# Down projection of a decoder layer: a third buffer for rounded values, four output banks, and clamps six units ahead of the additions

## What is computed

```python
def _quant_act_int8(x):
    amax = jnp.maximum(jnp.quantile(jnp.abs(x), 1.0 - 0.005), 1e-5)
    s = 127 / amax
    return jnp.clip(jnp.round(x * s), -128, 127) / s

def _quant_w_ternary(w):
    gamma = jnp.mean(jnp.abs(w)) + 1e-5
    return jnp.clip(jnp.round(w / gamma), -1.0, 1.0) * gamma

h = layernorm(x, ln_g, ln_b)
h = einsum('btd,hd->bth', _quant_act_int8(h), _quant_w_ternary(w1))   # up, 256 -> 1024
h = gelu(h)
out = einsum('btd,hd->bth', _quant_act_int8(h), _quant_w_ternary(w2)) # down, 1024 -> 256
x = x + (x + out)          # this part; x already holds the two stages before
```

## Time and profile before

| | us |
|---|---|
| median of 3 runs (lowest 1035.44, highest 1038.0) | 1035.82 |
| the profiled execution, its time | 1035.35 |
| its span, from the first to the last instruction | 1033.5 |
| VectorE's first instruction of the down projection starts at | 980.90 |
| last addition starts at | 1029.88 |
| last output DMA is issued at | 1031.35 |

### The profile page before, as it was taken

The page is one execution under the profiler, slowest core; times in us unless marked ns, Lnnn a source line. Parts: engine busy times, 40 slices in busy tenths (PEclk is TensorE's granted clock), DMA queues, the critical chain, the costliest instruction groups (busy, mean ns, idle before and its releaser), DMA issues.

```text
span 1033.5 us, 19418 instructions
## 1 busy us (share of the span) xinstructions
PE 880.8 (85%) x6218; PEld 674.9 (65%) x6225; DVE 867.2 (84%) x2448; ACT 659.6 (64%) x1663; POOL 545.7 (53%) x499
## 2 busy tenths in 40 slices
PE   7798999999989999999899899888999922995275
PEld 7586777777777777877777677655666621542164
DVE  4689899999999989889998879856677787899887
ACT  4677677776667756757666566345677651894095
POOL 6355476476456646644664554355678870880000
PEclk9899999999999989989998899999999975998599
DMA  9800000000000000002100000140420000000012
GB/s 163 138 3 10 6 6 11 7 7 10 8 7 8 10 6 6 8 9 80 55 11 7 6 6 10 29 125 21 155 79 1 1 1 1 1 1 1 1 67 97
DMA packets 28572, 30.49 MB, mean 30 GB/s; under 512 B 5548, under 2 KB 23864, under 8 KB 28472
## 3 DMA queue, kind: packets, MB, share of 16 engines
q1 hardware_dynamic: 28256, 29.12, 11.3%
q10 hardware_dynamic: 216, 0.14, 0.0%
HBM read 20.85 MB, written 4.19 MB: 24 GB/s over the span
## 4 chain that ended last, share of the span: by engine, by line
DVE 43%; PE 40%; issue 9%; ACT 4%; POOL 3%; DVEq 0%; ACTq 0%; POOLq 0%
PE ps L1862 6%; DVE arena L1283 5%; DVE arena L1291 5%; PE ps L2048 4%; DVE arena L1344 3%; PE ps L1932 3%; DVE arena L1269 3%; DVE arena L1272 3%; PE psY L1900 3%; PE psX L2069 3%; PE psY L2069 2%; PE ps L2247 2%; DVE arena L1336 2%; PE psG L2048 2%; DVE arena L1264 2%
## 5 line engine op out<-in xcount | busy, mean ns | idle before, releaser
L509 POOL TENSOR_SCALAR_AFFINE_SELECT arena<-arena 128x2048 f32<-128x2048 f32 x32 | 64.4, 2013 | 269.2 <-DVE arena L1272 262.7
L524 POOL TENSOR_TENSOR work<-work,half 128x16 f32<-128x16 f32 x32 | 93.8, 2931 | 2.7
L1924 PE MATMUL ps<-work 32*128 32x256 f32 x512 | 84.6, 406 | 10.2 <-ACT arena L713 10.1
L513 POOL TENSOR_SCALAR_AFFINE_SELECT arena<-arena 128x2048 f32<-128x2048 f32 x32 | 92.1, 2877 | 2.2
L678 ACT ACTIVATE arena<-ps,nparity 32x256 f32<-32x256 f32 x124 | 51.1, 457 | 63.8 <-PE ps L1862 63.4
L1924 PEld LDWEIGHTS ps<-work 32*128 32x128 f32 x512 | 54.7, 186 | 45.4 <-issue 27.1
L713 ACT ACTIVATE arena<-ps 128x512 f32<-128x512 f32 x128 | 68.9, 589 | 14.1 <-PE ps L1924 13.7
L1862 PE MATMUL ps<-work,arena 128*128 128x64 f32 x496 | 61.4, 277 | 19.3 <-DVE work L1308 19.2
L1862 PEld LDWEIGHTS ps<-work,arena 128*128 128x128 f32 x496 | 58.7, 193 | 28.8 <-issue 28.6
L1900 PE MATMUL psY<-work,arena 128*128 128x96 f32 (+1 forms) x512 | 69.1, 301 | 5.6 <-DVE arena L1362 5.6
L1900 PEld LDWEIGHTS psY<-work,arena 128*128 128x128 f32 x512 | 67.5, 216 | 6.4 <-DVE arena L1362 6.4
(11 more groups left out here) (344 smaller groups left out, 2548.7 us busy)
## 6 DMA issues: line engine op xcount, KB each, us to landing
arena<-in_mask_BxSxS_ik SPq DMA_DIRECT2D x8, 1024.0 KB, 6.8
xs<-arena SPq DMA_DIRECT2D x256, 16.0 KB, 1.8
arena<-in_ctx SPq DMA_DIRECT2D x8, 512.0 KB, 4.3
out<-xs SPq DMA_DIRECT2D x32, 128.0 KB, 1.7
arena<-in_x SPq DMA_DIRECT2D x8, 288.0 KB, 18.0
arena<-in_L_ffn_w SPq DMA_DIRECT2D x2, 1024.0 KB, 22.0
arena<-in_x SPq DMA_DIRECT2D x16, 96.0 KB, 6.4
arena<-in_L_attn_w_qkvb SPq DMA_DIRECT2D x2, 512.0 KB, 5.0
```

What stands on the lines that cost most here:

```text
L509: G.affine_select(out=keys, in_=keys, compare_op=ALU.is_ge, fill=0.0, base=0, pattern=[[0, NH], [1, P]], channel_multiplier=-1).then_inc(h ...
L513: G.affine_select(out=pairs, in_=pairs, compare_op=ALU.is_ge, fill=0.0, base=0, pattern=[[0, NH], [-CT, B], [0, CT]], channel_multiplier=1 ...
L524: own(G.tensor_tensor(root, length, half, ALU.pow))
L1924: last = M.matmul(ps[(2, 0)[r % 2]][:, f * 2 * P:(f + 1) * 2 * P], kq[j % 4][rows, f * P:(f + 1) * P], qe[rows, f].rearrange("p e t -> p ( ...
```

## The change

`gq` gets a third buffer, in the space of `hq` and `hqT`. Block i uses buffer i % 3, and the writers of unit u wait only from u = 12 on, for block i - 3. The output banks are four, `psX`, `psY`, `ps[0]`, `ps[1]`, and unit n waits for the addition of unit n - 4. VectorE clamps units 1, 0, 3, 2, 4, 5 first, and then for each n unit n + 6 before it adds unit n. No instruction is added or removed but waits; what each computes is the same.

```diff
         hq = [take_work(FF // 2).bitcast(BF16) for _ in range(2)]
         hqT = [take_work(FF // 2).bitcast(BF16) for _ in range(2)]
+        assert at[0] == third_block + 2 * FF
+        gq.append(work[:, third_block:at[0]].bitcast(BF16))
...
+        def down_bank(n):
+            return (psX, psY, ps[0], ps[1])[n % 4][:, 0:D]
...
             def quantised_gelu(u):
                 act.wait_ge(gr_ready, on_act(u))
-                if u >= 8:
-                    act.wait_ge(down_mm, 4 * (u // 4 - 1))
-                A.activation(gq[u // 4 % 2][:, u % 4 * FF:(u % 4 + 1) * FF], gT[:, u * FF:(u + 1) * FF], ACT.Copy,
+                if u >= 12:
+                    act.wait_ge(down_mm, 4 * (u // 4 - 2))
+                A.activation(gq[u // 4 % 3][:, u % 4 * FF:(u % 4 + 1) * FF], gT[:, u * FF:(u + 1) * FF], ACT.Copy,
                              bias=-ROUND).then_inc(ga_ready, 1)
...
             def clamped(u):
-                t, q = gT[:, u * FF:(u + 1) * FF], gq[u // 4 % 2][:, u % 4 * FF:(u % 4 + 1) * FF]
+                t, q = gT[:, u * FF:(u + 1) * FF], gq[u // 4 % 3][:, u % 4 * FF:(u % 4 + 1) * FF]
...
-                if u >= 8:
-                    v.wait_ge(down_mm, 4 * (u // 4 - 1))
+                if u >= 12:
+                    v.wait_ge(down_mm, 4 * (u // 4 - 2))
...
             def added(n):
                 v.wait_ge(down_mm, n + 1)
                 xt = xs[:, n, :]
-                V.scalar_tensor_tensor(xt, psO[n % 2], deq[:, 1:2], xt, ALU.mult, ALU.add).then_inc(out_ready, 1)
+                V.scalar_tensor_tensor(xt, down_bank(n), deq[:, 1:2], xt, ALU.mult, ALU.add).then_inc(out_ready, 1)
...
-            for u in (1, 0, 3, 2):
+            for u in (1, 0, 3, 2, 4, 5):
                 clamped(u)
             for n in range(NT):
-                if n + 4 < NT:
-                    clamped(n + 4)
+                if n + 6 < NT:
+                    clamped(n + 6)
                 added(n)
...
                 if r == 0:
                     pe.wait_ge(gd_ready, 4 * (i + 1))
-                if n >= 2:
-                    pe.wait_ge(out_ready, n - 1 + C)
+                if n >= 4:
+                    pe.wait_ge(out_ready, n - 3 + C)
                 for f in range(FC):
                     first = f * 512 + r * P
-                    last = M.matmul(psO[n % 2], gq[i % 2][:, first:first + P], w2t[:, f, :], start=f == 0, stop=f == FC - 1)
+                    last = M.matmul(down_bank(n), gq[i % 3][:, first:first + P], w2t[:, f, :], start=f == 0, stop=f == FC - 1)
                 last.then_inc(down_mm, 1)
```

More of the change, by code:

```diff
@@ L270, in decoder @@
         gq = [t.bitcast(BF16) for t in (cand, cand2)]
+        third_block = at[0]
         hq = [take_work(FF // 2).bitcast(BF16) for _ in range(2)]
         hqT = [take_work(FF // 2).bitcast(BF16) for _ in range(2)]
+        assert at[0] == third_block + 2 * FF
+        gq.append(work[:, third_block:at[0]].bitcast(BF16))
         spare = take_work(NT * FF // SEG * 2)
```

## The result

The changed kernel takes 1032.05 us, the median of six runs, beside 1037.89 for six runs of the kernel before in the same series. The ratio is that of the means, 1032.45 and 1037.41: 0.9952, with a 95% interval of 0.9931 to 0.9974. In the series of experiment 12 one run of the kernel before took 1161.57 us, in a slower state at a mean granted clock of 0.731, and no number here includes it. The changed kernel is faster, by 0.26% to 0.69%.

What follows compares the result with a forecast made beforehand. Three engines waiting in a ring bound the down projection; the last clamp gains 4.5 us, SyncE's output loop leaves 2.45. Forecast 1033.4 us (72%), 0.24% below 1035.82; own range 1032.4 to 1034.6, 8 in 10: 1031.2 to 1036.2.

Steps and rivals of the forecast that it cites:

- The pace of a block: Down projection: without waits, a block takes 5.12 us on ScalarE and VectorE alike, where it took 5.60.
- The last clamp: VectorE's last clamp in the down projection ends 4.5 us earlier, at 1021.6: 0.80 + 3.99 - 0.3 for ScalarE waits.
- Six ahead: VectorE clamping six units ahead in the down projection loses its waits for matmuls and gains overlap, together 3.99 us.
- third buffer: Down projection: it removes ScalarE's wait for a buffer TensorE has just left, 0.38 to 1.0 us a block.
- Four banks: TensorE in the down projection: two banks would make units wait for later additions; four leave 0.0 to 0.1 us, hidden.
- SyncE: End of span: seven late output DMAs at 1.09 us a loop turn, last issue at 1028.88; 2.45 of 4.5 us gained.
- Rival (a): SyncE at the end can go faster than 1.09 us, so the whole 4.5 us come: 1031.3 us; chance 10%.
- (b): Down projection's pace stays at 5.6 us a block, 1.5 us slower than now: 1037.3 us; chance 5%.
- (c): Down projection gain eaten piecemeal, VectorE waiting for ScalarE 0.25 to 0.4 us a block: 1035.8 us; chance 8%.
- Rival (d): TensorE's clock falls to half behind the joined pause in the down projection, 1.53 us a unit: near 1041 us; chance 5%.
- range for 8 in 10: Whole kernel's time lies between 1031.2 and 1036.2 us, reaching to rivals (a) and (c).
- faster by over 0.3%: Whole kernel's time falls below 1032.7 us, by rival (a) or the forecast's lower edge; chance 0.25.

Runs made afterwards that it cites:

- experiment 12: Changed kernel, output loop written out, each quarter-block multiplied once clamped over eight banks, first block in old order: 1029.88 us, ratio 0.9932 to before; stage 46.02.
- experiment 1: Changed kernel with VectorE clamping four units ahead as before, third buffer and four banks kept: 1035.3 us, ratio 0.9998 to before; stage 53.67 us.
- experiment 6: Changed kernel with clamps four ahead, plus four useless matmuls in TensorE's pause before each block but the first: 1035.13 us in one run; stage 52.60 us.
- experiment 4: Changed kernel with only the new order, six units ahead, and two buffers and two banks: 1048.55 us in one run; stage 64.97 us.
- experiment 10: Changed kernel without its third buffer: two buffers, six units ahead, four banks; 1035.56 us in one run, stage 51.18 us.
- experiment 9: Changed kernel with two output banks instead of four, three buffers and six units ahead kept: 1031.86 us in one run; stage 49.86 us.
- experiment 2: Changed kernel with SyncE's output loop written out as 32 waits and 32 DMAs with constant addresses: 1029.97 us, ratio 0.9944 to before; stage 46.92 us.
- experiment 7: Kernel before the change with only SyncE's output loop written out: 1034.94 us, ratio 0.9996 to before; stage 51.77 us.
- experiment 11: Changed kernel with clamps eight units ahead, not six: 1034.83 us in one run; stage 52.33 us.
- experiment 8: Changed kernel, clamps five ahead, output loop written out, each quarter-block multiplied once clamped over eight banks: 1031.77 us, ratio 0.9956 to before; stage 48.26 us.
- experiment 5: The changed kernel again, unaltered, with 12 runs against 29 of the kernel before: 1032.07 us, ratio 0.9967; stage 50.0 us.
- experiment 3: Changed kernel with clamps five units ahead, not six: 1034.09 us, ratio 0.9983 to before; stage 49.03 us.

## Why the prediction was right, and where not

**The pace of a block.** Forecast 5.12 us for VectorE and ScalarE alike; measured 5.11 on ScalarE, and L1817 holds VectorE for 0.34, the end that I took. Right.

**The last clamp.** Forecast 1021.6, that is 40.7 into the stage; measured 40.58. The 0.3 us that I added for handovers from ScalarE did not come, or only as 0.1 once. The clock had no part in it: it stood at 1.00 from 986.9 to past the last matmul at 1027.6.

**Six ahead.** Experiments 1 and 6 show that the storage without the order gains nothing, and experiment 4 that the order can't stand without storage. My text costed the third buffer by ScalarE's waits alone. Experiments 6 and 10 show what it is worth: nothing with the old order (there with the banks, and the pause filled), 1.2 us with the new, all at the eighth unit.

**Four banks.** I wrote that two would make matmuls wait, and that four hide it. Both are right (experiment 9), yet the banks don't pay here: SyncE is later than the wait.

**SyncE.** The step that decided: 1.09 us a turn, seven late DMAs, the last issue 3.0 us behind the last addition's end. Measured: 1.08, seven, 2.96. Experiments 2, 7 and 11 take the loop away, take it away without the change, and add two late DMAs (2.47 us later: two turns of 1.08 and the 0.31 that the step to a new outer turn adds). Rival (a) is out: the end did not follow the additions. The time alone would have pointed the wrong way, for the measured 1032.05 lies nearer to its 1031.3 than to my 1033.4.

**Rivals (b) and (c)** did not occur: no wait of VectorE for ScalarE stands in the changed kernel's waits of this stage. Experiment 11 has one of 0.80 us, so ScalarE was close behind.

**Rival (d), the clock.** Not in this stage of the changed kernel, where the pause is 1.44 us, but in experiment 1, with 1.93; with the pause filled (experiment 6) both the falls and the extra time were gone. My evidence against it, a pause of 1.94 in the attention stage at 1.00, was one execution, and too weak. The same pause stands in all fourteen traces, and in six of them (after, experiments 1, 7, 8, 11 and 12) the clock fell to 0.50 within 0.4 us of its end, for 3.4 us. In the changed kernel's own trace the same eight matmuls then took 3.66 us, not 1.99:

```profile
833.08 3.66 PE L2075 MATMUL psX<-arena 128*128 128x256 f32 x8 [1.95 <-ACT arena L953]
```

The size was off too. My unit at half clock, 1.53 us, was near (1.60 measured), but I had priced a whole stage of such units; the clock fell for a block at a time, and cost 0.94 us, not 6. By the Trainium skill ("TensorE: Matmul & The Clock Gate", section "A second HAM failure mode: psum-queue depth-cycling") a kernel that cycles through banks with short pauses can swing between the two levels; experiment 1 agrees with that, the changed kernel does not.

**The time.** Forecast 1033.4, which is 2.45 us less, with the stage 2.45 shorter; measured 1032.05, and the stage 2.64 shorter. The stage is right for the reasons given. The time agrees in part by luck. It lies in the range for 8 in 10 (1031.2 to 1036.2) but under the forecast's own (1032.4 to 1034.6), and the base moved: the median before was 1035.82 in the three runs that I had and 1037.89 in six. Less the same 2.45, the second would have given 1035.4. In relative terms I forecast 0.24%; the two series measured 0.48% (0.26% to 0.69%) and 0.33% (0.12% to 0.55%).

Here lies the one step that failed: I gave medians half a microsecond, from two of three runs. Single runs spread over nine. The part ahead of the stage is what varies: the stage began between 978.2 (experiment 5, mean granted clock 0.938) and 984.48 (experiment 12, clock 0.926), in kernels whose instructions ahead of it are the same. One part of that is the fall behind the pause of the attention stage: it made eight matmuls 1.67 us longer, and the six executions that have it begin the stage at 982.47 in the mean, the other eight at 980.79. The changed kernel's profile has it and that of the kernel before does not: that may be most of the 2.44 us by which the stage began later. For these reasons the chance of 0.25 for faster by over 0.3% was too small for a forecast of 0.24%.

**What stays open.** By the means the changed kernel is 5.0 and 3.5 us faster, more than the 2.6 of the stage, and 2.64 (a ratio of 0.9975) lies just outside the first interval. I don't take it for a second gain, since the other kernels with several runs show no common surplus. Their means lie 5.9, 2.0, 4.5 and 6.6 us below before in experiments 2, 3, 8 and 12, for stages shorter by 5.7, 3.6, 4.3 and 6.6; in experiment 7, 0.7 for 0.8; and experiment 1 was 0.2 slower with a stage 1.1 longer. But the runs don't exclude a microsecond outside the stage.

## What to carry to other kernels

When an edit lets an engine finish early, follow each result to its last DMA: work that was moved behind other work arrives in a burst, and the burst is served at the pace of the issuing queue's loop. A written-out output loop was worth more (3.04 us) than the edit that it stood behind (2.64), and only 0.83 without that edit. With the loop left as it was, looking ahead four, five, six and eight units gave stages of 52.6 (experiment 6), 49.0, 50.0 and 52.3 us: the best depth is where the waits are just gone, and each further step only lengthens the burst. And banks that spare TensorE a short wait can merge it into a longer one; behind two of five such merged pauses the clock fell.

## What the runs showed of the hardware

- A turn of SyncE's loop with computed addresses took 1.08 to 1.09 us, of which the issuing instruction took 0.34. Written out, issues of 128 KB that were late followed each other in 0.49 us. They landed after a median of 1.7 us all the same (1.9 for the last five of experiment 12).
- TensorE's granted clock fell to 0.50 for 3.4 us behind two of five pauses of 1.93 us in experiment 1, four of six of 2.15 us in experiment 4, and one pause of 1.95 us of the attention stage in six of fourteen executions. Pauses that looked alike had a fall behind them or not. It fell behind none of 48 pauses of 1.42 to 1.47 us in this stage, and none of seven that fillers had cut to 1.04.
- The way from an addition's end to its DMA's issue was 0.34 us through the loop's register instructions and 0.03 us with a constant address.
